# Routed expert results written plainly instead of added in DRAM, and summed in the kernel's last stage

## The reference

```python
gate_logits = x @ W_gate                      # 8 experts
top_w, top_idx = jax.lax.top_k(gate_logits, 2)
top_w = softmax(top_w)
for e in range(8):
    h = gelu(x @ W_in[e] + b_in[e])           # 128 -> 512
    y = h @ W_out[e] + b_out[e]               # 512 -> 128
    out = out + combine[..., e, None] * y     # combine: the weight of e for the token, or 0
x = _layernorm(x + out)
```

## Time and profile before

| | |
|---|---|
| median of 3 runs | 1410.42 us (1410.33 to 1412.01) |
| profiled execution, its own time | 1410.33 us |
| its span | 1408.2 us |
| PE busy | 88% of the span |
| DVE, ACT, POOL busy | 67%, 47%, 37% |
| TensorE clock granted, mean | 0.956 of full speed |

### The profile page before, as it was taken

One profiled execution on the slowest core, in us unless ns is written; L12 is line 12 of the kernel. 1 busy time (PEld: TensorE's weight loads), 2 busy tenths in 40 slices (PEclk: granted clock), 3 DMA queues, 4 the chain that ended last, 5 costly groups with the idle time before them and its releaser, 6 DMA issues. The chain is left out here.

```text
span 1408.2 us, 45352 instructions
## 1 busy us (share of the span) xinstructions
PE 1244.9 (88%) x16752; PEld 764.5 (54%) x16753; DVE 943.2 (67%) x1984; ACT 660.6 (47%) x1321; POOL 518.2 (37%) x509
## 2 busy tenths in 40 slices
PE   7589999999999978999999999999999967299990
PEld 4244444444444433457475656556465635199990
DVE  5668888788877842276867767685868556456664
ACT  4256676666766664242425252333324231055554
POOL 7311211212112211032534436161534344278785
PEclk9789999999999998999999999999999988599995
DMA  6453112121121223030404031131303050244555
GB/s 194 125 190 106 49 47 61 51 58 48 48 61 53 58 75 122 29 76 25 103 16 109 0 84 41 41 84 32 98 7 90 9 156 2 53 58 63 67 63 187
DMA packets 95006, 99.91 MB, mean 71 GB/s; under 512 B 16096, under 2 KB 76640, under 8 KB 94752
## 3 DMA queue, kind: packets, MB, share of 16 engines
q1 hardware_dynamic: 75808, 81.47, 20.6%
q0 software_dynamic: 13568, 12.13, 5.5%
q10 hardware_dynamic: 5504, 4.46, 1.0%
HBM read 49.84 MB, written 27.87 MB: 55 GB/s over the span
## 5 line engine op out<-in xcount | busy, mean ns | idle before, releaser
L1487 DVE TENSOR_REDUCE arena<-banks 128x4 f32<-128x512 f32 (+3 forms) x336 | 343.7, 1068 | 94.7 <-PE banks L1256 90.3
L1422 ACT ACTIVATE arena<-banks 128x512 f32<-128x512 f32 x576 | 304.9, 603 | 166.0 <-PE banks L1256 160.9
L1256 PE MATMUL banks<-arena 99*32 99x512 bf16 (+7 forms) x6144 | 337.0, 331 | 30.3 <-DVE arena L1487 12.1
L1256 PEld LDWEIGHTS banks<-arena 96*32 96x32 bf16 (+1 forms) x6144 | 151.4, 97 | 191.2 <-ACT arena L1422 69.3
L450 PE MATMUL banks<-arena,h 128*128 128x512 f32 x512 | 226.7, 593 | 2.4 <-DVEq L395 1.0
L1624 POOL TENSOR_SCALAR_AFFINE_SELECT arena<-arena 128x512 f32<-128x512 f32 x128 | 79.9, 637 | 383.1 <-ACT arena L1422 369.7
L1323 PE MATMUL banks<-arena 128*32 128x512 f32 (+3 forms) x1536 | 153.7, 490 | 11.2 <-POOL arena L1624 11.0
L450 PEld LDWEIGHTS banks<-arena,h 128*128 128x128 f32 x512 | 94.7, 190 | 110.0 <-issue 105.2
L598 ACT ACTIVATE arena<-banks,sh 128x512 f32<-128x512 f32 x64 | 44.0, 687 | 215.9 <-PE banks L450 215.9
L1015 POOL DMA_INDIRECT best<-arena x72 | 117.4, 1630 | 42.8 <-issue 25.8
L466 POOL TENSOR_TENSOR arena<-arena 128x4 f32<-128x4 f32 x23 | 23.4, 1017 | 267.0 <-DVE arena L464 267.0
(11 more groups left out here) (172 smaller groups left out, 1761.5 us busy)
## 6 DMA issues: line engine op xcount, KB each, us to landing
arena<-arena SPq DMA_DIRECT2D x160, 128.0 KB, 2.3
arena<-k_parts SPq DMA_DIRECT2D x96, 96.0 KB
arena<-rows SPq DMA_DIRECT2D x72, 65.0 KB
arena<-q_parts SPq DMA_DIRECT2D x64, 64.0 KB
k_parts<-arena SPq DMA_DIRECT2D x24, 128.0 KB, 3.2
q_parts<-arena POOLq DMA_DIRECT2D x24, 128.0 KB, 3.0
arena<-q_parts SPq DMA_DIRECT2D x32, 96.0 KB
best<-arena SPq DMA_DIRECT2D x12, 256.0 KB, 3.0
```

The costliest lines, as they stand in the source:

```text
L1256: ins = nc.tensor.matmul(dst[c:c + 32, :], lhs[:, c:c + 32], rhs, start=start, stop=stop, skip_group_check=True)
L1422: nc.scalar.activation(pe_[:, s % NSLOT, :], score[s % NBANK], ACT.Exp, scale=SCALE0)\
L1487: nc.vector.tensor_reduce(mx[:, 1 if k0 else 0, qt, hs[0]:hs[-1] + 1], src, AX.X, ALU.max)\
```

## The change

The rows come back by a plain write, so `best` needs no first content: x3 goes to a tensor of its own (`rest_d`), and the clears, their zero source and the waits for them go. The last stage then sums three parts instead of two: SP loads x3 during the expert stage (into `o_t`), and both halves of `best` at the end, pair by pair, now in runs of one token row (512 bytes); POOL adds the two halves, DVE adds that to x3. The negation moves from POOL to DVE. POOL's power and product of chunk c - 1 come behind its sum of chunk c. ACT issues the output's DMAs itself. The eight padding DMAs of L885 move from the end of the attention stage to its beginning, behind the loads of the later weights (`LATE`).

```diff
-        best_v = best[0:TOPK * NT, :].rearrange("(r b p h e) k -> r b h p e k", r=TOPK, b=B, p=P, h=2)
-        plain_v = best[0:NT, :].rearrange("(b c p) k -> c p b k", b=B, p=P)
+        best_v = best[0:TOPK * NT, :].rearrange("(r b c p) k -> r c p b k", r=TOPK, b=B, p=P)
...
-                plain_v[bass.ds(c, 1)].rearrange("c p b k -> p (c b) k"), x3), line="out")
+                rest_d[bass.ds(c, 1)].rearrange("c p b k -> p (c b) k"), x3), line="out")
...
             if me == "sp":
-                for g in range(NE):
-                    e.dma_start(rows[NE * REGION + g * P:NE * REGION + (g + 1) * P, :],
-                                a["padding"][(NE + g) * P:(NE + g + 1) * P, :]).then_inc(s_pad, 16)
                 e.wait_ge(s_ta, QC * NU)
...
-                    in_=y_g[:, k, :], in_offset=None, compute_op=ALU.add).then_inc(s_back[k], 16)
+                    in_=y_g[:, k, :], in_offset=None).then_inc(s_back[k], 16)
...
             tiles(0, False)
+            if me == "sp":
+                for c in range(T // P):
+                    e.dma_start(parts[c][0], rest_d[c]).then_inc(s_rest, 16)
...
-                if me in ("sp", "act"):
-                    r = 0 if me == "sp" else 1
-                    e.dma_start((one, two)[r], best_v[r, c // 2, c % 2]).then_inc(s_parts[c], 16)
+                if me == "sp":
+                    for r, dst in enumerate((one, two)):
+                        e.dma_start(dst, best_v[r, c]).then_inc(s_parts[c], 16)
+                if me == "pool":
+                    e.wait_ge(s_parts[c], 32)
+                    nc.gpsimd.tensor_tensor(one, one, two, ALU.add).then_inc(s_both, 1)
                 if me == "dve":
-                    e.wait_ge(s_parts[c], 32)
-                    nc.vector.tensor_tensor(one, one, two, ALU.add).then_inc(s_d, 1)
+                    if c == 0:
+                        e.wait_ge(s_rest, 16 * NC)
+                    e.wait_ge(s_both, c + 1)
+                    nc.vector.tensor_tensor(total, total, one, ALU.add).then_inc(s_d, 1)
...
+                    nc.vector.tensor_scalar(less_e[:, c, :], mv_e[:, c, :, 0], -1.0, None, ALU.mult).then_inc(s_var4, 1)
+                def scales(c):
+                    e.wait_ge(s_var4, 2 * c + 2)
                     nc.gpsimd.tensor_tensor(rstd_e[:, c, :], var_e[:, c, :], minus_half[:, :], ALU.pow)\
                         .then_inc(s_rstd4, 1)
-                    nc.gpsimd.tensor_scalar(less_e[:, c, :], mv_e[:, c, :, 0], -1.0, None, ALU.mult)\
-                        .then_inc(s_rstd4, 1)
-                    e.wait_ge(s_rstd4, 3 * c + 2)
+                    e.wait_ge(s_rstd4, 2 * c + 1)
                     nc.gpsimd.tensor_tensor(less_e[:, c, :], less_e[:, c, :], rstd_e[:, c, :], ALU.mult)\
                         .then_inc(s_rstd4, 1)
+                if me == "pool":
+                    for k in ([c - 1] if c else []) + ([c] if c == NC - 1 else []):
+                        scales(k)
...
             for n in LATE:
                 e.dma_start(late[n][:], a[n]).then_inc(s_late, 16)
+            for g in range(NE):
+                e.dma_start(rows[NE * REGION + g * P:NE * REGION + (g + 1) * P, :],
+                            a["padding"][(NE + g) * P:(NE + g + 1) * P, :]).then_inc(s_pad, 16)
...
-                if isinstance(u, int) and u in (1, NU - 2):
-                    clear(u > 1)
...
-            nc.gpsimd.memset(att_c, 0.0).then_inc(s_zero, 1)
```

More of the change, by code:

```diff
@@ L1037, in experts @@
             tiles(NJ - 1, True)
-            NC = 2 * B
-            if me in ("sp", "act"):
+            NC = T // P
+            if me == "sp":
                 for k in range(XG):
@@ L1044, in experts @@
             for c in range(NC):
-                one, two = parts[c]
-                if me in ("sp", "act"):
-                    r = 0 if me == "sp" else 1
-                    e.dma_start((one, two)[r], best_v[r, c // 2, c % 2]).then_inc(s_parts[c], 16)
-                if me == "dve":
-                    e.wait_ge(s_parts[c], 32)
-                    nc.vector.tensor_tensor(one, one, two, ALU.add).then_inc(s_d, 1)
-                    e.wait_ge(s_d, 4 * c + 1)
-                    for t in range(4):
-                        ins = nc.vector.bn_stats(st_e[:, c, t, 0:6], one[:, t, :])
+                total, one, two = parts[c]
@@ L1055, in experts @@
                     ins.then_inc(s_d, 1)
-                    e.wait_ge(s_d, 4 * c + 2)
-                    for t in range(4):
+                    e.wait_ge(s_d, 3 * c + 2)
+                    for t in range(B):
                         ins = nc.vector.bn_aggr(mv_e[:, c, t, :], st_e[:, c, t, 0:6])
                     ins.then_inc(s_d, 1)
-                    e.wait_ge(s_d, 4 * c + 3)
-                    nc.vector.tensor_scalar(var_e[:, c, :], mv_e[:, c, :, 1], EPS, None, ALU.add).then_inc(s_d, 1)
@@ L1073, in experts @@
                 if me == "act":
-                    e.wait_ge(s_rstd4, 3 * c + 3)
-                    for t in range(4):
-                        ins = nc.scalar.activation(two[:, t, :], one[:, t, :], ACT.Identity,
+                    e.wait_ge(s_rstd4, 2 * c + 2)
+                    for t in range(B):
+                        ins = nc.scalar.activation(one[:, t, :], total[:, t, :], ACT.Identity,
                                                    bias=less_e[:, c, t:t + 1], scale=rstd_e[:, c, t:t + 1])
@@ L1078, in experts @@
                     ins.then_inc(s_norm, 1)
-                if me == "sp":
                     e.wait_ge(s_norm, c + 1)
-                    e.dma_start(out_v[c // 2, c % 2], two).then_inc(s_out, 16)
-            if me == "sp":
+                    e.dma_start(out_v[c], one).then_inc(s_out, 16)
+            if me == "act":
                 e.wait_ge(s_out, 16 * NC)
@@ L1208, in unit @@
                     stacks(u + 2, p, 1)
-            def clear(part):
-                e.wait_ge(s_zero, 1)
-                n = (NZERO - NT // 512) // 2
-                for k in range(NT // 512 + n * part, NT // 512 + n * part + n):
-                    e.dma_start(best[512 * k:512 * k + 512, :].rearrange("(p e) k -> p e k", p=P), att_c)\
-                        .then_inc(s_zeroed, 16)
             def first_in(b, s_in, done):
                 e.wait_ge(s_att[0], 16 * 2 * HQ * done)
-                e.wait_ge(s_zeroed, 16 * (NZERO - NT // 512))
                 e.dma_start(sum_c[:, b, :], sum_v[:, b, 0:P]).then_inc(s_in, 16)
```

23 lines of the change are left out of this document (13 added, 10 removed).

## The result

The changed kernel takes 1420.62 us at the median of four executions (1420.27 to 1421.26), the kernel before 1411.22 us (1410.33 to 1412.5): ratio 1.0066, 95% interval 1.0049 to 1.0084. It is slower, as forecast, but by 9.4 us instead of 5.2, and 0.6 us beyond the range. The profiled execution took 1413.79 us, with a span of 1412.0 us, and is shorter than the four that were timed then.

A forecast was written before the change was run, and what follows sets the result against it. The prediction took PE to pace the expert stage and DVE the tail, where POOL would become the bound. Tail +8.4, earlier first add -1.7, stage -1.0, clear -0.5 gave +5.2 us on 1410.33: 1415.6 us, range 1411.5 to 1420.0.

The forecast's parts named there:

- PE paces the expert stage: Expert stage: PE's rate with the loop's sequencing sets a tile each 2.00 us, and POOL's writes only follow.
- Rival 1: Expert stage: POOL's writes pace the tiles, so plain writes gain 7.1 us instead of 1.0, giving 1409.5 us; chance 0.17.
- The saving of 1.0 us: Expert stage: the plain write saves 0.6 us of late rows and a little in short waits, taken as 1.0 us.
- From the last tile to the first add: Between expert and last stage: shorter write and faster first pair of loads bring the first add 1.7 us earlier.
- The tail's new owner: Last stage: POOL becomes the bound, 3.3 us a chunk where DVE took 2.12, costing 8.4 us.
- Rival 2: Last stage: POOL's power and add run undisturbed beside DVE, cost 5.4 us, time 1412.6; chance 0.04 alone.
- rival 3: Last stage: DVE's add waits for POOL's power or add at the ports, 4 us more, 1419.8 us; chance 0.15.
- Then 4.1 us as before: Kernel's end: ACT, output DMA and end follow the last product by 4.1 us, unchanged.
- 0.3 us for the output's shorter runs: Kernel's end: output runs of 512 bytes in place of 2 KB cost 0.3 us.
- Clears and padding: Attention stage: dropping the twelve clears and moving the eight paddings costs or saves 0; 5.1 us if the paddings' cover were gone.
- The 0.5 us for POOL's clear: Kernel's start: without POOL's clear of the zero source, everything behind moves up by about 0.5 us.
- The sum: Whole kernel: +8.4 - 1.7 - 1.0 - 0.5 = +5.2 us on 1410.33, so 1415.6 us.

The follow-up runs named there:

- b1: The kernel before, unchanged, timed and profiled again: 1409.24 us, ratio 0.9988.
- c1: The kernel before with plain row writes only in the last of nine rounds (8 tiles): 1408.13 us in one execution, kernel before there 1409.68.
- d3: The kernel before with plain row writes in the first round alone (8 of 72 tiles): 1413.4 us in one execution, kernel before there 1410.86.
- c3: The changed kernel with both adds of a chunk on DVE, POOL keeping power and product: 1414.09 us, ratio 1.0043.
- first session: Four runs on one chip: the changed kernel again and three versions with one side edit undone each: 1418.36 to 1420.75 us, kernel before there 1410.59.
- d1: The changed kernel, unchanged, on another chip: 1415.48 us, ratio 1.0043.
- b3: The changed kernel without POOL's add of the two halves, leaving out each token's second result: 1409.0 us, ratio 0.9991.
- b4: The changed kernel with the add of the two halves shared, half on POOL and half on DVE: 1411.8 us, ratio 1.0013.
- a3: The changed kernel with the last stage's result reads and output writes back in runs of 2 KB: 1420.75 us, ratio 1.0064.
- b2: The kernel before with plain instead of accumulating row writes, nothing else changed: 1409.51 us, ratio 0.999.
- a2: The changed kernel with the eight padding DMAs back at the end of the attention stage: 1419.9 us, ratio 1.0056.
- a1: The changed kernel, unchanged, timed and profiled again: 1419.47 us, ratio 1.0055.
- c4: The kernel before with plain writes, no clears, and x3 added in the expert's bias operation, two parts in the last stage: 1409.44 us, ratio 1.0001.

## Why the prediction was right and where it was wrong

- **PE paces the expert stage: right.** POOL's writes became 0.65 us shorter and its idle time took all of it. Rival 1 (a period below 1.96 us) did not come: 141.5 / 71 = 1.99 us. The saving of 1.0 us is borne out in size, and comes at least in part from where it was put: with plain writes in the loop the stage is 141.1 to 141.9 us in eight of the profiles, with accumulating ones 142.3 to 143.8 us in all four. In the stage, PE's wait for rows that arrive late is 0.6, 1.9, 0.9 and 1.4 us in those four (before, b1, c1, d3) and absent from those with every write plain, but for 0.3 us in c3. The first session and d1 are the exceptions, with 143.1 to 145.9 us and plain writes.
- **From the last tile to the first add: right.** 6.7 us, from 8.8: 2.1 us less where I had 1.7. The first pair took 3.59 us for the 3.6 assumed; the rest came between write and issue, 2.34 us from the start of the write where I had 2.72.
- **The tail's new owner: right in mechanism and nearly in size.** POOL bounds it, add 1.26 us (taken: 1.28), power 1.42 beside DVE's add, period 3.09 us for 3.3. Its parts: hand-over 0.04 instead of 0.08, rest of the power 0.87 for 0.90, product and the gap behind it 0.15 for 0.25, add 1.26 for 1.28; together 0.2. From the first add to the end of the last product it was 26.4 us, for 26.75. b3 and b4 show the add as the cause. Rival 2 failed on the 1.42 us. Of rival 3 a side part came: DVE's variance is held under POOL's add, 0.72 us in the first chunk that meets one and 1.03 to 1.07 in the others. DVE's add itself never waited (0.69 us in all eight), and b4 and c3 show that it doesn't even beside a power under way. The hold made the negation late and left POOL idle 0.18 us behind its add. Whether a power that was ready at once would have gone ahead of DVE's add, and saved its wait for it, no run shows; a version with the power ahead of POOL's add was not tried.
- **"Then 4.1 us as before": this step failed.** From the end of the last product to the span's end it was 6.2 us. The prediction took the distance as ACT's work, the output DMA and the end, with 0.3 us for the output's shorter runs, a term that no row shows (a3 puts it at 0.2), and these came nearly as assumed: ACT is done 4.4 us behind the last product, where SP was at 3.9 before. Beside them lay a second chain, POOL's closing DRAIN of 4.05 us, ending 0.1 us ahead of SP's last wait; the plain write makes it 6.2 us, and 1.6 us of that stand behind the end of all other work. b2 has it without any other part of the change. With 6.2 in place of 4.4 (the 4.1 and 0.3) and the terms as measured, the tail costs 39.6 - 31.9 = 7.7 us instead of 6.7. That 1.0 us is more than the 0.6 by which the median lies beyond the range.
- **Clears and padding: right where zero, unproven where not.** a2 shows the padding's place as free, to within 3 us. The 0.5 us for POOL's clear can't be seen: the last copy of the attention stage starts at 543.0 us in the profile of after, 545.3 in that of before, but from 543.8 to 548.6 in the others, with no order by kernel.
- **The sum.** +5.2 was forecast; +7.7 for the tail and -1.0 for a stage without late spots make 6.7 us. Measured were 9.4, 8.9 (a1) and 4.6 us (d1). The median lies 5.0 us above the forecast's 1415.6. Of these, 0.8 us are the kernel before, which was then timed at 1411.22 instead of 1410.42, and 1.0 is shown as the tail (1.8 of the end, less the smaller errors). The remaining 3.2 us are not settled. Late results of PE, 2.5 to 3 us in the profiles of the first session, are of that size, but the four timed executions of the result have no profile, and the time ahead of the experts varies by more.
- **Where a number would have come right, it would have been by luck.** The profiled execution lies 3.5 us above that of before, with a tail 7.7 us longer, since it happened to reach the experts 3.1 us earlier. d1's 4.6 us, close to the 5.2, also stands beside a tail that is 7.5 us longer. For the kernels with plain writes on the other three chips (b2 to b4, c3, c4, d1) the timed difference to before is 0.6 to 3.3 us smaller than the tail's, in the first session 0.1 to 2.6 us larger. The tail's is the one difference that every profile shows.

## What to carry to other kernels

A faster instruction on an engine that follows another one gives idle time; the page's chain can still name it. An extra full-width operand in a closing stage costs its sequence on whichever of DVE and POOL owns the stage. Moving the whole add to POOL gained nothing here (3.09 us a chunk against 2.92 with both on DVE), for its add is slower and its power waits for DVE's; halving it gained a little (2.65). Look first for a stage that has slack and already holds the operand (here 0.04 us a tile instead of 1.0 us a chunk). And when a kernel's end is priced as "as before", check what each engine's sequencer does in its last microseconds; a DRAIN that ends together with the last landing is a second critical chain without a wait.

## What the runs showed of the hardware

- POOL's closing DRAIN starts with its last instruction and lasts 4.05 us (3.93 in d3) where the looped indirect writes to `best` accumulate and 6.21 to 6.22 us where they are plain; those of SP and ACT take 0.01 us when they come last. The Trainium skill, "VectorE: DVE Perf Modes", section "The DRAIN you can't avoid", calls the DRAINs around a program constant at about 12 ns on all engines; that agrees with SP's 7 ns and not with POOL's 4052 and 6214, and the measurement decides.
- An indirect DMA of 128 rows keeps POOL for 0.95 us, for 1.55 to 1.60 with an accumulation.
- POOL's add of two 128x512 f32 operands takes 1.26 us and one of 128x256 0.72 us, DVE's 0.69 and 0.42 us. A DVE operation of four elements, 0.17 us alone, is held to 1.03 us beside POOL's add, and POOL's power of four elements, 1.01 us alone, to 1.42 us when it starts under DVE's. DVE's add is not lengthened by a power that started before it (0.69 us, b4 and c3).
